# Five more row units through DRAM, and three reorderings around them, in an fp32 feed-forward, attention, feed-forward kernel

## The reference

```
q = (x @ Wq.T)  32 heads of 128;   k, v = (x @ Wk.T), (x @ Wv.T)  8 heads of 128
q = rmsnorm(q) * q_norm_w;         k = rmsnorm(k) * k_norm_w
scores = q @ k.T / sqrt(128) + causal ALiBi bias       4 query heads share one key head
x = x + softmax(scores) @ v @ Wo.T
```

## Time and profile before

| what | before |
|---|---|
| time, median of 3 runs | 1201.85 us (1201.79 to 1204.67) |
| time of the profiled execution | 1203.9 us |
| its span | 1202.6 us |
| TensorE busy | 1184.3 us, 98% |
| VectorE, ScalarE, GpSimd busy | 73%, 63%, 55% |
| attention slots | 263.0 to about 976 us |
| blocked units | 48 of 64 |

### The profile page before, as it was taken

How to read it: one execution, slowest core, us unless ns; L and a number is a source line. 1 busy time by engine, 2 the same in 40 slices (tenths; PEclk the granted TensorE clock), 3 DMA queues, 4 the chain that set the end, 5 groups by cost and what they waited for, 6 DMA issues and landing times.

```text
span 1202.6 us, 18492 instructions
## 1 busy us (share of the span) xinstructions
PE 1184.3 (98%) x6128; PEld 1036.5 (86%) x6128; DVE 877.8 (73%) x2071; ACT 756.8 (63%) x1764; POOL 666.6 (55%) x538
## 2 busy tenths in 40 slices
PE   6999999999999999999999999999999999999999
PEld 5888888899998899898899899899898888888887
DVE  7876665687787677787787787787787878655555
ACT  4554443347677777777778778778767765544442
POOL 4796661535676635835824824825824344965540
PEclk9999999999999999999999999999999999999999
DMA  6152333213234145245244244344244120211101
GB/s 239 41 177 93 108 107 105 88 53 110 87 125 133 53 145 159 78 145 157 81 145 149 87 146 136 103 145 150 88 145 132 49 70 1 87 55 53 53 18 70
DMA packets 69310, 125.24 MB, mean 104 GB/s; under 512 B 8096, under 2 KB 33600, under 8 KB 68192
## 3 DMA queue, kind: packets, MB, share of 16 engines
q1 hardware_dynamic: 68976, 123.76, 31.9%
q10 hardware_dynamic: 240, 0.30, 0.1%
HBM read 78.42 MB, written 45.61 MB: 103 GB/s over the span
## 4 chain that ended last, share of the span: by engine, by line
PE 86%; POOL 4%; issue 4%; ACT 3%; DVE 3%; DMA 1%; SPq 0%; POOLq 0%; DVEq 0%; ACTq 0%
PE bank L406 19%; PE bank L408 19%; PE bank L407 19%; PE bank L720 5%; PE bank L518 4%; PE bank L513 4%; PE bank L512 4%; PE bank L739 3%; PE bank L734 3%; PE bank L735 2%; ACT prob L1125 1%; PE bank L434 1%; POOL rows L1922 1%; POOL o_l L1790 1%; PE bank L701 1%
## 5 line engine op out<-in xcount | busy, mean ns | idle before, releaser
L1125 ACT ACTIVATE prob<-prob,neg_top 128x128 f32<-128x128 f32 (+3 forms) x256 | 141.5, 556 | 72.7 <-DVE neg_top L1607 68.0
L1922 POOL TENSOR_TENSOR rows<-rows,row_root_y 128x640 f32<-128x640 f32 x64 | 81.8, 1278 | 173.5 <-DVE row_root_y L1278 172.2
L1916 POOL TENSOR_TENSOR square<-rows 128x640 f32<-128x640 f32 x64 | 79.9, 1265 | 137.3 <-DVE rows L1650 113.1
L1790 POOL TENSOR_TENSOR w_l_late<-raw_late,w_h_late 128x512 fp32r<-128x512 f32 (+1 forms) x59 | 91.7, 1568 | 71.7 <-ACT w_h_late L856 71.6
L1134 ACT ACTIVATE prob<-prob,inverse 128x128 f32<-128x128 f32 (+3 forms) x252 | 121.0, 556 | 1.7 <-DVE inverse L1612 1.7
L1354 DVE SCALAR_TENSOR_TENSOR x_rows<-bank,x_rows 128x512 f32<-128x512 f32 x111 | 74.9, 687 | 44.3 <-PE bank L518 44.3
L1625 DVE TENSOR_TENSOR probT_l<-bank,probT_h 128x512 fp32r<-128x512 f32 x160 | 100.5, 675 | 3.6 <-ACT probT_h L1140 3.5
L1140 ACT CAST probT_h<-bank 128x512 fp32r<-128x512 f32 x160 | 84.5, 596 | 26.1 <-PE bank L720 26.1
L408 PE MATMUL bank<-o_h,oT_l 128*128 128x512 f32 x256 | 100.9, 394 | 0.0
L406 PE MATMUL bank<-o_h,oT_h 128*128 128x512 f32 x256 | 100.5, 392 | 0.2 <-DVE oT_l L1631 0.2
L407 PE MATMUL bank<-o_l,oT_h 128*128 128x512 f32 x256 | 100.6, 393 | 0.0
(11 more groups left out here) (246 smaller groups left out, 3805.6 us busy)
## 6 DMA issues: line engine op xcount, KB each, us to landing
x_ring<-x_between SPq DMA_DIRECT2D x64, 256.0 KB, 2.7
row_turns<-row_blocks SPq DMA_DIRECT2D x48, 320.0 KB, 2.2
turned_rows<-row_turns SPq DMA_DIRECT2D x192, 80.0 KB, 2.1
x_between<-x_ring SPq DMA_DIRECT2D x56, 256.0 KB, 2.1
raw_late<-w_qkv SPq DMA_DIRECT2D x16, 768.0 KB, 5.0
raw_early<-ffn_w SPq DMA_DIRECT2D x21, 512.0 KB, 4.3
scaled<-raw_early SPq DMA_DIRECT2D x21, 512.0 KB, 2.7
raw_late<-scaled SPq DMA_DIRECT2D x21, 512.0 KB, 3.7
```

The lines of the kernel that those rows point to most:

```text
L1125: last = act.activation(p, p, ACT.Exp, bias=neg_top[:, h:h + 1], scale=-1.0, accum_out=total[:, h:h + 1])
L1790: return pool.tensor_tensor(lo, raw, hi.bitcast(F32), ALU.subtract)
L1922: pool.tensor_tensor(row, row, by, ALU.mult).then_inc(rows_normed, 1)
```

## The change

The units 21, 29, 37, 45 and 53 (the sixth of groups 2 to 6) become blocked: TensorE transposes them no longer, VectorE blocks them in slot n-2, SyncE stores and fetches them, ScalarE turns them at the start of the slot before and GpSimd makes their rests there. So there are 53 blocked units.

Beside this: ScalarE makes the high parts of the next unit's rows ahead of its probabilities in the slots with at 3 (19, 27, 35, 43, 51, 59). In slots 20, 28, 36, 44 and 52, ScalarE makes t3's high part, takes a product (6), copies the turned probabilities and only then makes those of t4 and b22; VectorE adds product 2 between two root steps and makes the rest of the turned probabilities right behind the roots, ahead of the ring's addition and the blocking of unit n+2; GpSimd makes t3's rest ahead of the norm of unit n+2.

```
-PLAIN_ROWS = 6, 10, 13, 14, *range(21, UNITS, B * TB)
+PLAIN_ROWS = 6, 10, 13, 14
...
# ScalarE, slot(n)
-                if n == 0:
+                rows_first = n == 0 or no_turn(n) and at == 3
+                if rows_first:
 
                     turn_rows(n + 1)
                 probabilities(n)
...
-                if n and not (no_turn(n) and n % 2 == 0):
+                if not rows_first and not (no_turn(n) and n % 2 == 0):
                     turn_rows(n + 1)
...
                 if half_behind:
                     take_left(ahead - 1)
                     split_qkv(g + 1, *splits[:1])
+                elif no_turn(n) and at == 4:
+                    half_behind = True
+                    split_qkv(g + 1, *splits[:1])
+                    take_sum(ahead, 6)
...
# VectorE, slot(n)
-                if n % 2 == 0:
+                turned_first = no_turn(n) and n % (B * TB) == 4
+                if turned_first:
+                    pair_roots(n + LEAD - 2, 1, lambda: add_products(ahead, 2))
+                    turn_probabilities(n)
+                elif n % 2 == 0:
                     pair_roots(n + LEAD - 2)
-                if paired(ahead) and not sums_first:
+                if paired(ahead) and not sums_first and not turned_first:
...
-                if n:
+                if n and not turned_first:
                     turn_probabilities(n)
...
# GpSimd, slot(n)
+                splits = list(QKV_WHEN[g + 1 >= SEVEN_FROM].get(at, ())) if g < HKV - 1 else []
+                if rows_early(n) and at == 4 and splits:
+                    split_qkv(g + 1, splits.pop(0))
                 if n + 2 < UNITS and n != UNITS - 3:
                     norm_rows(n + 2)
...
-                if g < HKV - 1:
-                    split_qkv(g + 1, *QKV_WHEN[g + 1 >= SEVEN_FROM].get(at, ()))
+                split_qkv(g + 1, *splits)
```

## The result

| what | before | after |
|---|---|---|
| median of 4 runs | 1203.11 us | **1214.32 us** (1213.3 to 1215.23) |
| ratio to before | | **1.0091**, 95% interval 1.008 to 1.0103 |
| span of the profiled execution | 1202.6 us | 1212.6 us |
| slots 19 to 21 and their four counterparts, sum | 175.99 us | 188.04 us |

The change is slower, and the time lies outside the forecast range of 1197.5 to 1208. The five stretches took 12.05 us more (forecast: 1.9 more); the rest of the kernel took 2.0 us less, of which slot 57, which no longer begins with a wait, gave 1.0.

The account below looks back on a forecast made before the run. TensorE, 98% busy, was taken as the bound, but its gain of about 8 us is given back at slot 22 by unit 22's chain: +1.2 us plus w gives +1.9, so 1201.85 + 1.9 = 1203.8 us, range 1197.5 to 1208.

Parts of the forecast that it names:

- the stalls at slots 21, 28 and 36: TensorE idle for `qT_l`, 0.63 us before slot 21 and 0.91 before slot 28; the change would remove them.
- ScalarE's wait w: ScalarE at 3 waits for unit 20's rows to land: 0.6 us in group 2, 0.15 in group 4.
- rival B: ScalarE waits for unit 20's DMA in slots 19, 27, 35, 43, 51: slower, 1210 or 1206.3 us; chance 0.26.
- rival A: TensorE's gain stands, GpSimd's row norm not last to arrive: -8 us, 1194, or -4, 1198; chance 0.16 together.
- GpSimd's own line: GpSimd's work from t1's high part through t3's rest to unit 22's norm, which ends 10.96 us after that part.
- the part on GpSimd: GpSimd at 4: 3.53 us of new work fills its 2.16 us wait for the roots; norm ends 503.85, against 502.48.
- the two waits above: VectorE's two rests of unit 20 each wait out one GpSimd instruction of 1.86 us, the last ending near 490.6.
- 5 x 35.43 + 0.75: Slots 19 to 21 in five groups: slot 22 begins 35.43 us after slot 19, plus w of 0.6 + 0.15.
- 5 x 26.23: End of unit 22's norm on GpSimd, 26.23 us after slot 19's start, in five groups.
- 7.5 + 1.7 = 9.2: From unit 22's norm to ScalarE's use of its rows 7.5 us, then 1.7 to its scores in slot 22.
- The forecast's upper bound for this term, +3.4: Norm to use holds two transfers, median 2.1 us each; two late ones of 1.7 us make +3.4.
- up to 2 us in slot 21: Scores 21 and `oT_l` come 0.9 us later on VectorE; TensorE's stall lies inside slot 22's, so counted at nothing.

Follow-up runs that it names:

- the last experiment above: Kernel before, ScalarE turning rows first at 3, GpSimd's squares moved to slot 19, plus VectorE's new order in slots 12, 20, 28, 36, 44, 52: 1217.07 us.
- norm first, squares early: Changed kernel with GpSimd's rest of t3 behind the norm again and its squares of units 22 and 23 in slot 19: 1206.27 us, ratio 1.0029.
- blocked only: Kernel before with units 21, 29, ... taken out of `PLAIN_ROWS` and no reordering: 1209.93 us, ratio 1.0051.
- VectorE's old order: Changed kernel with `turned_first = False`: addition behind the roots, turned probabilities last; 1222.62 us, ratio 1.0167.
- filler writes: Kernel before plus four GpSimd MEMSETs of an unused corner behind t4's mixing in slots 12, 20, 28, 36, 44, 52: 1207.24 us, ratio 1.0044.

## Why the prediction was wrong, point by point

**Right.** Slot 20 takes 10.05 to 10.07 us without its transpositions (10.03 forecast), and the stalls at slots 21, 28 and 36 are gone. ScalarE's wait w is 0.75 us in group 2 and 0.30 in group 3, none in the others (forecast 0.6, and 0.15 in one group); so rival B did not come. Slot 22's start is set by unit 22's rows, not by TensorE, in every group; so rival A did not come either. GpSimd's own line was summed up rightly as well: up to the end of t3's rest the forecast gives 24.90 us after slot 19's start, plus w, and the trace has 25.71, 25.25 and three times 24.93. (The terms as printed make 10.98, not 10.96.)

**The step that failed** is in the part on GpSimd: "The roots come 0.5 us later because of the addition between them, and no longer decide." They came at 26.4 to 27.2 us, 2.1 to 3.7 us later than in the same groups of before, and they do decide: GpSimd idles 1.53 us for them behind t3's rest, in every group. The addition itself costs 0.35 us (the last experiment above). I had the rule on two SBUF inputs and a row that showed it, and applied it to `qT_l` alone ("nothing more than the two waits above would be added"). Nine of the eleven root steps are instructions with two SBUF inputs as well, and the change laid GpSimd's reads over the first of them, without a gap until 503.13: two were held, for 2.85 us together. Filling an idle engine's wait was priced as free; here the filler held what the wait was for.

**The size.** The five stretches came to 188.04 us, where the forecast makes them 5 x 35.43 + 0.75 = 177.9. The norm ended at 28.51, 28.05 and three times 27.72 us, against 5 x 26.23 and the forecast's w of 0.75 in sum: 7.8 us more, of which 7.7 are the five waits of 1.53 us for the roots. From norm to slot 22 it took 9.3 to 9.9 us instead of 7.5 + 1.7 = 9.2: 2.3 us in sum, the second failed term. It was taken from one row with its wait for VectorE subtracted; in group 2 it is the 8.08 us from 505.92 to 514.00. The wait for VectorE did go, but from the store's issue to the use it took 7.13 us (506.87 to 514.00) instead of 6.61 (503.88 to 510.49); why the transfers took longer was not tested. The forecast's upper bound for this term, +3.4, holds it.

**Counted at nothing.** VectorE's delay of `oT_l` and the probabilities was put at "up to 2 us in slot 21", inside the stall at slot 22. The place and the size held, 2.1 to 2.4 us in each group, and slot 22 still begins 1.7 us after the rows' use. But the larger part, 1.31 to 1.87 us, is a wait for the turned probabilities, whose rest the forecast had ready "as soon as the roots are out" without pricing late roots; `oT_l` is 0.6. That this delay would cost 1 us or more if the stall at slot 22 were absent was not borne out: norm first, squares early has no such stall, and TensorE waits there 1.4 us for t3's rest and no more than 0.2 us for VectorE.

**The Trainium skill's** advice (Perfetto Trace Analysis, "Identifying the Most-Contended Engine") to optimize the engine with the highest occupancy first was no guide to what taking work away is worth. The section would have TensorE's headroom judged not by its matmuls but, among others, by the busy share of its weight loads; at 86% that is still the highest of the engines. TensorE lost 2.7 us of work, and the kernel 11 us; 4.9 us were to be had by moving two instructions of GpSimd, 55% busy, and one step of ScalarE, which took away waits of TensorE and none of its work.

## What to carry to other kernels

Before a reading GpSimd instruction is moved into an idle stretch, look at what VectorE does in it: short steps with two SBUF inputs are held to the end of each GpSimd instruction, and show as long **busy** times rather than waits. Compare the durations of one and the same small instruction across a trace: 0.17 against 1.41 and 1.78 us was the sign here. Then look for what is queued behind the held steps, since it can be more than one thing: here the norm and unit 22's rows, the turned probabilities, and the plain unit's rests, and it differed from kernel to kernel which of them TensorE felt. And when a number comes out as forecast, check that the wait you meant is the one that changed.

## What the runs showed of the hardware that was not expected

MEMSETs on GpSimd, which read nothing, held VectorE's TENSOR_SCALAR steps (0.55 us; 1.36 us for one that began under the mixing) and none with two inputs (0.17). And TensorE's clock: in slot 21 of group 2 of the changed kernel it did 0.67 us of work in 2.70 at a granted 1.00, and then 3.70 us followed at 0.54, near the lower level of 1.2 GHz; the 384-column matmuls started 0.32 us apart (506.29, 506.61) and 0.17 apart at the full clock (512.41, 512.58). There it cost next to nothing, since the rows of unit 22 came later still.

Its price shows in norm first, squares early, where TensorE waits 1.39 us for t3's rest in slots 45 and 53 alike. The windows of these two slots, and of two microseconds inside the second:

```profile
773.50:785.48 11.98, 10.50 (x63) 9.19 (x61) 7.71 (x24) 8.55 (x22) 8.73 (x7) 1.00 0.35 108
864.20:877.85 13.65, 12.08 (x63) 10.51 (x61) 8.62 (x26) 8.56 (x22) 8.66 (x7) 0.87 0.34 112
...
871.00:873.00 2.00, 2.00 (x7) 1.63 (x6) 0.56 (x1) 1.48 (x4) 2.00 (x3) 0.50 0.64 164
```

The same 63 matmuls and the same wait, 13.65 - 11.98 = 1.67 us apart: one slot kept its clock, the other fell to 0.50. It fell in one such slot of five here, in three of five in blocked only and in four of five in VectorE's old order, where TensorE waits twice in the slot (up to 1.9 and 1.6 us). In filler writes it fell in none, with waits of up to 1.46 us. What makes it fall is not settled. A wait of 1.4 us in TensorE's stream can thus cost 3, and that makes the times of kernels with such waits uneven: by the estimates above it is most of the loss of blocked only and as much as VectorE's old order adds.
